# Three decoder stages on one Trainium2 core: fewer readerless TensorE products at the start, and the first and last three turns in another order

## The reference

```python
x = _layernorm(x + attn(x))      # causal, 16 heads of 64, 8 key/value groups, then W_out and a bias
x = _layernorm(x + xattn(x))     # 8 heads of 64 over at most 5 allowed of 77 context rows, with its own layer norm
x = _layernorm(x + ffn(x))       # silu(x @ wg.T) * (x @ wu.T) @ wd.T, 768 hidden, integer weights / 127
```

## Time and profile before

| | |
|---|---|
| median of three executions | 2044.49 us |
| the profiled execution, its span | 2043.62 us, 2041.8 us |
| TensorE busy | 2013.7 us (99%) |
| weight loads of TensorE busy | 1850.6 us (91%) |
| VectorE, ScalarE, GpSimd busy | 1542.5, 1321.9, 375.9 us |
| mean granted TensorE clock | 0.996 of full |

### The profile page before, as it was taken

How to read it: one execution, slowest core, us unless ns; L and a number is a source line. 1 busy time by engine, 2 the same in 40 slices (tenths; PEclk the granted TensorE clock), 3 DMA queues, 4 the chain that set the end, 5 groups by cost and what they waited for, 6 DMA issues and landing times.

```text
span 2041.8 us, 50701 instructions
## 1 busy us (share of the span) xinstructions
PE 2013.7 (99%) x18228; PEld 1850.6 (91%) x18228; DVE 1542.5 (76%) x5708; ACT 1321.9 (65%) x3992; POOL 375.9 (18%) x624
## 2 busy tenths in 40 slices
PE   9999999999999999999999999999999999999997
PEld 8899999999999999999999999999999999999886
DVE  6877777777777777777777777777777777777764
ACT  7866666666666666666666666666666666666642
POOL 3112111211212121112111112112121211121211
PEclk9999999999999999999999999999999999999998
DMA  5100000000000000000000000000000000000000
GB/s 163 32 8 22 19 12 21 8 22 19 22 12 18 11 19 22 19 12 19 11 22 19 12 21 8 22 19 21 12 18 11 19 22 18 12 16 14 14 6 11
DMA packets 49606, 41.19 MB, mean 20 GB/s; under 512 B 19536, under 2 KB 47568, under 8 KB 49360
## 3 DMA queue, kind: packets, MB, share of 16 engines
q1 hardware_dynamic: 49360, 37.96, 6.5%
HBM read 29.56 MB, written 8.39 MB: 19 GB/s over the span
## 4 chain that ended last, share of the span: by engine, by line
PE 96%; ACT 1%; DVE 1%; issue 1%; POOL 0%; POOLq 0%; DVEq 0%; ACTq 0%
PE gen L441 19%; PE gen L443 19%; PE gen L442 19%; PE s_ps L581 9%; PE z_ps L623 7%; PE gen L529 3%; PE pt_ps L602 3%; PE gen L538 3%; PE gen L542 3%; PE pt_ps L603 3%; PE z_ps L625 3%; PE pt_ps L607 3%; PE gen L509 2%; PE gen L500 1%; PE gen L553 1%; PE s_ps L635 1%
## 5 line engine op out<-in xcount | busy, mean ns | idle before, releaser
L967 ACT ACTIVATE SM<-SM,least 128x128 f32<-128x128 f32 (+1 forms) x1024 | 452.3, 447 | 33.2 <-DVE least L1492 33.2
L897 ACT ACTIVATE PT<-pt_ps 128x512 f32<-128x512 f32 (+1 forms) x512 | 238.1, 486 | 244.2 <-PE pt_ps L603 242.7
L1492 DVE CUSTOM_DVE_ANT_0 SM<-s_ps,causal 128x128 f32<-128x128 f32 (+1 forms) x1024 | 314.1, 351 | 14.9 <-PE s_ps L581 13.5
L1505 DVE TENSOR_SCALAR SM<-SM,total 128x128 f32<-128x128 f32 (+1 forms) x1024 | 280.2, 336 | 9.1
L1871 POOL TENSOR_TENSOR H_lo<-gated,H_hi 128x256 fp32r<-128x256 f32 x192 | 141.6, 744 | 513.9 <-ACT H_hi L897 513.7
L950 ACT ACTIVATE gated<-gen 128x256 f32<-128x256 f32 x192 | 73.6, 384 | 206.8 <-PE gen L443 204.4
L581 PE MATMUL s_ps<-KT,QT 64*128 64x128 f32 (+1 forms) x2048 | 201.5, 335 | 0.0
L967 ACT ACTIVATION_READ_ACCUMULATOR SM<-SM,least 128x1 f32 x1024 | 197.0, 192 | 0.0
L1469 DVE SCALAR_TENSOR_TENSOR gated<-gated,gen 128x256 f32<-128x256 f32 x192 | 80.8, 421 | 121.9 <-ACT gated L950 121.6
L623 PE MATMUL z_ps<-PT,Vt 128*64 128x256 f32 x1024 | 168.0, 399 | 0.0
L581 PEld LDWEIGHTS s_ps<-KT,QT 64*128 64x128 f32 x2048 | 147.5, 187 | 20.1 <-issue 6.7
(11 more groups left out here) (185 smaller groups left out, 6514.1 us busy)
## 6 DMA issues: line engine op xcount, KB each, us to landing
xT_in<-in_xT SPq DMA_DIRECT2D x32, 256.0 KB, 2.9
x_in<-in_x SPq DMA_DIRECT2D x32, 256.0 KB, 2.8
out<-rows SPq DMA_DIRECT2D x32, 256.0 KB, 2.2
ctx_in<-in_ctxT SPq DMA_DIRECT2D x32, 77.0 KB, 2.9
mask_in<-in_maskT SPq DMA_DIRECT2D x32, 77.0 KB, 2.7
SX<-in_wq SPq DMA_DIRECT2D x1, 512.0 KB, 6.1
rows<-in_wv SPq DMA_DIRECT2D x1, 512.0 KB, 7.0
xwk<-in_xwkv SPq DMA_DIRECT2D x1, 512.0 KB, 7.9
```

The costliest lines, as they stand in the source:

```text
L897: return act.activation(o, i, ACT.Copy)
L967: ins = act.activation(part, part, ACT.Exp, scale=-1.0, bias=least[:, i % 4, n:n + 1], accum_out=total[:, i % 4, n:n + 1])
L1492: ins = dve.tensor_tensor_reduce(SM[:, i % 4, at:at + keys], s_ps[bank][:, col:col + keys], causal[:, S - keys:S], -SCALE, -3 * NEG, ALU.a ...
L1505: ins = dve.tensor_scalar(part, part, total[:, i % 4, n:n + 1], None, ALU.mult)
```

## The change

Nothing is computed differently and no instruction of the 29 turns between changes. On every engine the orders of the first three and the last three turns are written anew, and FIRST_ITEMS and LAST_ITEMS with them. Ahead of the first product there were twelve calls of `warm` (24 products) and one more between the first two fills; there are four (8 products). In the last three turns there were 16 calls and there are 12, in other places.

The head of TensorE's list in the first turns:

```diff
-                t.warm(0, 0), (0, 4), (0, 10), (0, 11), (0, 1), (0, 5)
-                t.warm(0, 6), (0, 15), (0, 7), (0, 14), (0, 8), (0, 3)
+                t.warm(0, 0), (0, 3), (0, 5), (0, 2)
                 s.fill("nQ0")
-                t.warm(0, 2)
                 s.fill("nK0")
-                t.fill("aK1")
                 t.scores(0)
                 t.fill("aQ1")
+                t.fill("aK1")
+                t.fill("aXK")
                 t.fill("aQ2")
-                t.fill("aV0")
                 t.scores(1)
-                t.transposed("a", 0)
                 t.fill("aV1")
-                t.fill("aQ3")
+                t.transposed("a", 0)
+                t.fill("aV0")
                 t.scores(2)
                 t.transposed("a", 1)
-                u.fill("aXK")
+                t.fill("aQ3")
                 t.values("a", 0)
                 t.values("a", 1)
                 t.transposed("a", 2)
                 t.scores(3)
                 t.transposed("a", 3)
+                t.values("a", 2)
                 t.fill("nK0")
-                t.values("a", 2)
+                t.fill("nQ0")
+                t.transposed("a", 4)
                 t.values("a", 3)
-                t.transposed("a", 4)
-                t.fill("nQ0")
+                u.scores(0)
+                t.transposed("a", 5)
                 u.fill("aQ1")
...
```

(Calls of `warm` stand on lines of their own in the code.) ScalarE's and VectorE's, and GpSimd's:

```diff
                 s.fill("nQ0")
                 s.fill("nK0")
                 split_high(4)
+                split_high(5)
                 u.split_context()
-                split_high(5)
+                t.exps(0, 0)
+                t.fill("aQ1")
+                split_high(6)
                 t.fill("aK1")
-                split_high(6)
-                t.fill("aQ1")
-                t.exps(0, 0)
                 t.exps(0, 1)
+                t.fill("aXK")
                 split_high(7)
+                t.fill("aQ2")
                 t.exps(1, 0)
-                t.fill("aQ2")
-                t.fill("aV0")
+                t.exps(1, 1)
                 split_high(8)
-                split_high(9)
                 t.probs_out("a", 0, 0)
-                t.exps(1, 1)
                 t.exps(2, 0)
                 t.probs_out("a", 0, 1)
+                split_high(9)
...
+                t.masked(0, 0)
                 split_low(4)
-                split_low(5)
-                t.masked(0, 0)
                 t.masked(0, 1)
                 t.masked(1, 0)
+                split_low(5)
                 t.masked(1, 1)
                 t.probabilities(0)
...
                 split_low(6)
+                u.context_low()
                 split_low(7)
                 split_low(8)
                 split_low(9)
                 t.x_low()
+                split_low(10)
                 u.x_bias()
-                u.context_low()
-                split_low(10)
                 split_low(11)
```

The last turns from the end of `t` on (TensorE):

```diff
                 t.fill("fDOWN1")
+                u.transposed("o", 6)
                 t.fill("fDOWN0")
-                t.warm(4, 16)
-                t.warm(4, 1)
+                t.warm(4, 19)
...
                 u.fill("fXOUT")
                 u.fill("oOUT0")
+                u.fill("oOUT1")
                 u.fill("fT3")
-                u.fill("oOUT1")
+                t.warm(4, 15)
                 u.fill("fFFN0")
                 u.fill("fFFN1")
                 u.fill("fFFN2")
                 u.fill("fFFN3")
-                t.warm(4, 10)
                 u.fill("oT10")
-                t.warm(4, 12)
-                t.warm(4, 9)
+                t.warm(4, 16)
                 u.fill("oT11")
                 u.fill("fFFN4")
                 u.fill("fFFN5")
                 u.fill("oXQ1")
                 u.fill("oXQ0")
-                t.warm(4, 2)
                 u.fill("oSIM10")
                 u.fill("oSIM00")
                 u.fill("fDOWN1")
-                u.fill("oXV")
                 u.fill("fDOWN0")
                 u.fill("oT200")
-                t.warm(4, 19)
-                t.warm(4, 15)
+                u.fill("oXV")
                 u.fill("oT201")
                 u.fill("oT211")
                 u.fill("oT210")
                 u.fill("oXPV0")
                 u.fill("oXPV1")
                 v.fill("fXOUT")
-                v.fill("fT3")
                 t.warm(4, 5)
                 t.warm(4, 22)
+                t.warm(4, 17)
+                t.warm(4, 1)
+                t.warm(4, 0)
+                v.fill("fT3")
                 v.fill("fFFN0")
...
                 v.fill("fFFN5")
                 t.warm(4, 14)
-                t.warm(4, 6)
-                t.warm(4, 0)
-                t.warm(4, 17)
-                t.warm(4, 4)
                 t.warm(4, 21)
+                t.warm(4, 10)
+                t.warm(4, 9)
                 v.fill("fDOWN1")
                 v.fill("fDOWN0")
```

More of the change, by code:

```diff
@@ L682, in first_turns @@
                 u.transposed("o", 6)
-                u.fill("aQ2")
+                u.fill("aK1")
                 u.transposed("o", 7)
+                u.fill("aXK")
                 u.values("o", 6)
@@ L687, in first_turns @@
                 u.scores(1)
-                u.fill("aV0")
                 u.fill("oOUT0")
                 u.fill("oOUT1")
-                u.fill("aK1")
+                u.fill("aV1")
                 u.transposed("a", 0)
-                u.fill("aV1")
-                t.fill("aXK")
+                u.fill("aV0")
+                u.fill("aQ2")
                 u.scores(2)
@@ L830, in last_turns @@
                 t.values("a", 5)
-                t.fill("oT201")
                 t.fill("oT211")
+                t.fill("oXPV0")
                 t.fill("oT210")
-                u.transposed("o", 6)
-                t.fill("oXPV0")
                 u.transposed("o", 7)
@@ L1076, in first_turns @@
                 u.z_high_out("o", 3)
-                u.fill("aQ2")
-                u.exps(0, 0)
-                u.exps(0, 1)
-                u.fill("aV0")
-                split_high(12)
-                u.exps(1, 0)
-                u.exps(1, 1)
-                split_high(13)
-                split_high(14)
-                u.fill("aK1")
-                u.exps(2, 0)
-                u.probs_out("a", 0, 0)
-                u.fill("aV1")
+                u.exps(0, 0)
+                split_high(12)
+                u.exps(0, 1)
+                u.fill("aXK")
+                u.exps(1, 0)
+                split_high(13)
+                u.exps(1, 1)
+                split_high(14)
+                u.fill("aV1")
+                u.probs_out("a", 0, 0)
+                u.exps(2, 0)
+                u.exps(2, 1)
+                u.fill("aV0")
+                u.fill("aQ2")
+                u.exps(3, 0)
                 u.probs_out("a", 0, 1)
-                t.fill("aXK")
-                u.exps(2, 1)
                 u.fill("oT10")
@@ L1310, in last_turns @@
                 u.context_exps(1)
+                u.fill("oT200")
                 u.fill("oXV")
                 u.fill("oT201")
-                u.fill("oT200")
                 u.fill("oT211")
@@ L1637, in first_turns @@
                 u.z_low_out("a", 0)
+                u.fill("oSIM00")
                 u.fill("oSIM01")
-                u.fill("oSIM00")
-                u.probabilities(4)
                 u.context_shift(0)
@@ L1643, in first_turns @@
                 u.context_probs(0)
+                u.probabilities(5)
                 u.context_probs(1)
-                u.probabilities(5)
+                u.z_low_out("a", 1)
                 u.masked(6, 0)
-                u.z_low_out("a", 1)
                 u.masked(6, 1)
@@ L1725, in last_turns @@
                 t.masked(1, 1)
+                t.probabilities(0)
+                t.z_low_out("o", 3)
                 t.x2()
-                t.z_low_out("o", 3)
-                t.fill("fT3")
-                t.probabilities(0)
-                t.probabilities(1)
-                t.masked(2, 0)
-                t.fill("oOUT0")
-                t.masked(2, 1)
+                t.masked(2, 0)
+                t.masks()
+                t.fill("oOUT0")
+                t.probabilities(1)
+                t.masked(2, 1)
+                t.fill("fT3")
                 t.fill("oOUT1")
@@ L1771, in last_turns @@
                 t.context_probs(1)
-                t.probabilities(6)
+                t.moments_3()
                 t.probabilities(7)
+                t.fill("oXPV0")
                 t.z_low_out("a", 2)
-                t.fill("oXPV0")
                 t.fill("oXPV1")
-                t.moments_3()
                 u.z_low_out("o", 3)
+                t.y()
                 u.fill("fXOUT")
                 u.moments_2()
+                u.masks()
                 u.x2()
                 u.fill("oOUT0")
-                t.y()
+                u.fill("oOUT1")
                 u.fill("fT3")
-                u.fill("oOUT1")
                 u.moments_1()
                 u.fill("fFFN0")
```

(10 more changed lines are left out.)

285 lines of the change are left out of this document (138 added, 147 removed), and 24 rows, old and new, of tables (FIRST_ITEMS, LAST_ITEMS).

## The result

The changed kernel takes 2038.51 us (median of 9 runs, 2035.75 to 2040.97) against 2043.35 us before (9 runs on the same chip, 2042.12 to 2045.43): ratio 0.9973, 95% interval 0.9965 to 0.9982. That is 4.8 us or 0.24% faster by the medians (0.27% by the ratio), just beyond the 0.2% that can be told from no change. The forecast was 2039.4. The profiled execution took 2038.91 us.

A forecast was written before the change was run, and what follows sets the result against it. TensorE was taken to bound the kernel, so only the first and last stages could gain: 2.2 + 2.9 = 5.1 us off the profiled 2043.62 gives 2038.5, and 0.87 more 2039.4 us; range 2034 to 2044 with rivals.

The forecast's parts named there:

- The start: First stage: `nQ0` begins 4.4 us earlier, `scores(0)` at 10.1; real lead 3.3 us, 2.0 after piece 6's landing.
- The lock: First stage: GpSimd's splits hold VectorE's divides; lead at `transposed(1)` taken as 1.5 us, from 0.2 to 3.6.
- my worst case: First stage: `probabilities(0)` and `probabilities(1)`, held by GpSimd's splits, end at worst at 22.9 and 29.4 us.
- my best: First stage: `probabilities(0)` and `probabilities(1)` are done at best by 20.3 and 25.7 us.
- rival D: First stage: lock makes TensorE wait over 3 us at `transposed(1)`, clock falls to 1.2 GHz; 2050 us; chance 0.08.
- From there to the first `turn_between`: First stage behind `transposed(1)`: waits can be filled or grow; +0.7 us, from -2 to +2.5.
- The last three turns: Turns `t`, `u` and `v` together: 2.9 us gained, from -0.5 to 5.
- 0.5 + 1.4: Last stage: 0.5 us gained in `t` (a readerless call goes) and 1.4 in `u` (fills and calls moved).
- I take 1.0: Turn `v`: five readerless calls in the wait ahead of T3 may keep the clock up; 1.0 us gained.
- The prediction's best case: Turn `v`: clock stays up, 24 records of two FFN fills give 2.2 us; 2.1 at best for `v`.
- Rival B: First stage gains only 0.5 us, lost to piece 6's landing and GpSimd's lock; last 1.5: 2042.5 us; chance 0.20.
- Rival C: Both stages: divides slip between the splits, clock stays up; 4.5 + 4 = 8.5 us gained, 2036; chance 0.18.

The follow-up runs named there:

- tail_full: Changed kernel with 14 more readerless calls (56 records) in waits of the last two turns: 2036.21 us, 0.9962 of the kernel before.
- act_order: Changed kernel with piece 6's split moved on ScalarE behind the copies of `aQ1` and `aK1` and `exps(0,1)`: 2041.83 us, 0.9994 of the kernel before.
- start12: Changed kernel with the old readerless calls put back (twelve ahead of `nQ0`, one behind it), new orders kept: 2043.5 us, 1.0000 of the kernel before.
- act_hold_mask: `act_hold` with GpSimd also waiting for the context mask ahead of `x_bias` and piece 11's split: 2039.0 us, 0.9978 of the kernel before.
- last_new: Kernel before with only the last three turns of the change: 2042.16 us, 0.9993 of the kernel before.
- start4: Kernel before with only the readerless calls at the start cut to four, old orders kept: 2042.29 us, 0.9992 of the kernel before.
- first_new: Kernel before with only the first three turns of the change: 2040.15 us, 0.9983 of the kernel before.
- hold: Changed kernel with GpSimd's splits of pieces 7 and 9 waiting for `probabilities(0)` and `probabilities(1)`: 2038.26 us, 0.9973 of the kernel before.
- act_hold: `act_order` with GpSimd's splits of pieces 7 and 8 waiting for `probabilities(0)` and `probabilities(1)`: 2038.14 us, 0.997 of the kernel before.
- start0: Changed kernel without any readerless call ahead of `nQ0`: 2041.05 us, 0.9985 of the kernel before.
- start12_hold: `start12` with GpSimd's splits of pieces 7 and 9 waiting for `probabilities(0)` and `probabilities(1)`: 2040.5 us, 0.9983 of the kernel before.
- best: Changed kernel with the edits of `act_hold_mask` and `tail_full` together: 2035.63 us, 0.9962 of the kernel before.

## Why the prediction was right, and where it was not

The time, 2038.5 against 2039.4 forecast, and the side were right, and so was the place: nothing in the middle, a gain in both ends. That the number is so close is in part luck: the first stage gave 3.2 us where I had 2.2, the last 1.6 where I had 2.9, and inside both stages too terms missed in opposite directions. By its steps:

- **The start.** Right. `nQ0` at 5.67 (5.65 forecast), `scores(0)` at 9.67 (10.1; the clock rose earlier than I took it, but of seven other kernels with this start and this order up to there six had it at 10.07 to 10.76, and only `tail_full` at 9.79), piece 6 split at 15.39 (15.45), `scores(1)` at 18.66 (18.5). Of the 5.3 us of lead 1.5 were the order, one fill less ahead of `scores(0)`, as the prediction says; the landing of piece 6 made the other 3.8 into 2.2. `act_order` shows that it is the landing: with the split out of the way, `scores(1)` is 1.5 us earlier.
- **The lock: right as a mechanism, mis-sized here.** I took the lead at `transposed(1)` as 1.5 us, in a range of 0.2 to 3.6, "nearer the bad end". In the profile `transposed(1)` waits for nothing: 29.89 - 26.07 = 3.8, less 0.3 for the order, is a lead of 3.5, at the good end. `probabilities(0)` ended at 22.2, near my worst case of 22.9. `probabilities(1)` ended at 25.5, at my best of 25.7: I had it due at 23.1, inside a split, and it began at 24.53, when ScalarE's high split of piece 9 left GpSimd idle until 25.70. I had said that GpSimd "may get in after the first" of the four operations. It does, and not only after the first: where GpSimd has work ready, it gets in behind every divide. At its worst it costs what rival D said: `start12` waits 3.27 us at `transposed(0)` and `act_order` 3.98 at `transposed(1)`, and behind both the clock is at 0.5 to 0.58, as D had it. D's mechanism was shown there, with another price: the stage 7.0 and 4.4 us longer than the changed kernel's, times of 2043.5 and 2041.8, not 2050, since the rest of the order keeps its gain. In the changed kernel it didn't come, for gaps of 0.55 and 0.99 us. The Trainium skill's rule on the lock ("SBUF — State Buffer", "SBUF: two separate sides") says that the lock is held for the whole instruction. The traces agree: no divide was held beyond the one GpSimd instruction beside it, 2.51 us at most. They show besides that the two engines take turns, so that a group of four divides can pay for four GpSimd instructions: 6.94 and 6.44 us were measured for groups of 1.01.
- **From there to the first `turn_between`.** I had +0.7 for it and it was -0.35: 3.5 us of lead came in, 3.17 went out, and `oOUT0`'s wait grew by 0.34, which fits. I had not read that the lock holds the mask operations; with those out of its way, piece 11's split binds `oOUT0` only 0.4 us earlier (`act_hold_mask`).
- **The last three turns.** The sum was 2.9; the two profiles show 1.6 and the median of `last_new` 1.46. Up to `v`'s `fXOUT` the gain was larger than forecast: it takes 2002.67 - 1891.55 = 111.1 us from the first scores of the last stage to there, before 2008.53 - 1894.61 = 113.9 (the row below is the kernel before's), so 2.8 against 0.5 + 1.4. FFN0 of `u` waits 1.06, the loss of 0.4 as said. The term that failed is `v`, "I take 1.0": from `fXOUT` to the end it took 2037.1 - 2002.67 = 34.4 us after and 2041.8 - 2008.53 = 33.3 before, a loss of 1.2 unrounded. The clock stayed up at T3 as hoped, but fell in `fXOUT` ahead of it and in FFN0 behind it. My 1.0 looked at one wait, and 1.73 and 1.50 us of waiting were left on both sides of T3. `tail_full` shows this: with those filled, the same stretch takes 2033.1 - 2001.45 = 31.65, 2.8 less.

```profile
2008.53 0.36 PE L441 MATMUL gen<-xwo_hi,H_hi 128*128 128x256 f32 x1 [1.51 <-DVE H_lo L1455]
```

  The other profiles set the 1.2 right: what makes most of it is whether `fXOUT` meets the low clock. Where its first record took 0.36 us or less, from there to the end is 33.3 us in the old order (before) and 33.0 to 33.9 in the new (six kernels); where it took 0.53 or more, 34.1 and 34.2 in the old order (`start4`, `first_new`) and 34.4 to 35.4 in the new (three kernels, the changed one among them). So like with like the new order of `v` brought nothing, and in all nine kernels with it the first two FFN fills ran at least in part at 1.2 GHz. The prediction's best case was also too large: it took 24 records at the low clock in these two fills, and the trace of the kernel before has 15, from 2018.12 to 2021.4 us, 1.4 us and not 2.2.

- **Rival B**, that the gain is lost again, is what `start12` and nearly what `start4` show; it did not happen because start and order fit each other. **Rival C** had half of the first stage's mechanism right (`probabilities(1)` slipped between the splits, `probabilities(0)` did not) and not the second: the clock did fall.

The tail's length varies between kernels whose tail is the same code, from 143.3 to 145.6 us over nine profiles, and so the 1.6 us of one pair of profiles is a draw. Most of it goes with the time that TensorE spends at 1.2 GHz in the last stage, added up from the granted clock in half microseconds up to 8 us before the end:

| order of the last turns | us at 1.2 GHz | last stage, us |
|---|---|---|
| old: before, `first_new` | 13.7 | 147.2, 146.9 |
| old: `start4` | 17.1 | 148.0 |
| new: changed, `act_hold_mask`, `hold`, `act_hold` | 13.7 | 145.6, 145.6, 144.8, 144.5 |
| new: `start0` | 10.2 | 144.7 |
| new: `start12`, `last_new`, `start12_hold`, `act_order` | 6.8 | 143.3, 143.4, 143.4, 144.7 |
| new with more readerless calls: `best`, `tail_full` | 3.4, 0 | 143.0, 142.0 |

At 13.7 us of low clock the new order is 1.3 to 2.7 us shorter than the old: that is what the order brings, in `t` and `u`. With less low clock the same order was up to 2.3 us shorter again. It is also why `start12` loses 7.0 us in its first stage and only 5.0 in the median. What decides in which waits the clock falls stays open.

## What to carry to other kernels

Ask of an earlier start where it is held next: here 3.8 us of lead became 2.2 at a load and 3.2 at the end, and the same start brought 1.3 us in the old order and 5.0 in the new. When a group of short VectorE operations meets a row of long GpSimd ones, price one GpSimd instruction for each of the short ones, not one for the group, and look for the gaps that other engines leave in it; making GpSimd wait for VectorE can be a gain. At the thin end of a kernel, price the clock over all the waits around a stretch: with a single one filled the clock still fell in its neighbours, filling them all brought 2.3 us.

## What the runs showed of the hardware beyond that

- GpSimd and VectorE took turns. A divide was never held by more than one GpSimd instruction (2.51 us at most), but behind each divide the next GpSimd instruction got in: four divides of 1.01 us in sum took 6.94 (`start12`, held by four), 6.44 (`act_order`, by three) and 4.14 (the changed kernel, by three, one of them short).
- It works the other way too: a GpSimd split that began at 19.53 while VectorE ran a low split from 19.16 for 1.22 us took 3.13 instead of 2.41 (`start12`).
- Operations as small as 128x2 are held as well: a count of masks took 1.81 us beside the split of piece 11 and 0.17 without it.
- The granted-clock column reads 1.00 in the first microseconds while the number of records in them (11 in 2 us, against 20 later) shows the lower level; in the tail, column and records agree (15 records in 3 us at 0.50).
- In the tail the clock fell among waits of 0.6 to 1.7 us, in the first stage (once it had risen) only behind the waits of 3.27 and 3.98 us; behind 2.31 us (before) and 2.37 us (`start4`) it stayed up there.
